# The first layer norm shared between ScalarE and VectorE, the receptance weights split inside the mix, and one block of transposes moved to the head of unit 18

## What is computed

```python
x = L0_attn_x                                   # (1, 2048, 512)
y = _layernorm(x)                               # plain norm
h = _layer_norm(y, ln1_g, ln1_b)                # the norm of the block
hh = _time_shift(h)                             # the token before
r = (h * tm_mr + hh * (1 - tm_mr)) @ Wr.T       # receptance
k = (h * tm_mk + hh * (1 - tm_mk)) @ Wk.T       # key
v = (h * tm_mv + hh * (1 - tm_mv)) @ Wv.T       # value
...
x = y + sigmoid(r) * wkv(k, v) @ Wo.T           # and so on:
                                                # channel mix, then SiLU-gated FFN
```

## Time and profile before

| | us |
|---|---|
| median of three runs | 1042.37 (1040.67 to 1045.35) |
| profiled execution, its own time | 1042.62 |
| its span in the profile | 1040.8 |
| TensorE busy | 1030.8 (99% of the span) |
| VectorE busy | 746.1 (72%) |
| GpSimd busy | 664.5 (64%) |
| ScalarE busy | 538.9 (52%) |

### The profile page before, as it was taken

One profiled execution on the slowest core, in us unless ns is written; L12 is line 12 of the kernel. 1 busy time (PEld: TensorE's weight loads), 2 busy tenths in 40 slices (PEclk: granted clock), 3 DMA queues, 4 the chain that ended last, 5 costly groups with the idle time before them and its releaser, 6 DMA issues.

```text
span 1040.8 us, 13820 instructions
## 1 busy us (share of the span) xinstructions
PE 1030.8 (99%) x4607; PEld 850.6 (82%) x4607; DVE 746.1 (72%) x1240; ACT 538.9 (52%) x902; POOL 664.5 (64%) x541
## 2 busy tenths in 40 slices
PE   8999999999999999999999999999999999999998
PEld 6777888888888888878888888888888888888887
DVE  7899866786576687586568577788689466666655
ACT  7866888857444445355354534333435344444442
POOL 7796673726676875777747565678683456665652
PEclk9999999999999999999999999999999999999999
DMA  9100325367867787989924565964945455445432
GB/s 349 59 21 0 60 66 118 102 204 266 329 219 292 266 277 245 353 310 313 284 99 164 196 227 172 239 236 142 298 164 196 152 169 177 149 153 162 160 103 81
DMA packets 98854, 197.09 MB, mean 189 GB/s; under 512 B 40160, under 2 KB 53344, under 8 KB 93920
## 3 DMA queue, kind: packets, MB, share of 16 engines
q1 hardware_dynamic: 74880, 146.84, 41.3%
q0 software_dynamic: 15168, 48.24, 15.1%
q10 hardware_dynamic: 8736, 1.14, 1.2%
HBM read 117.00 MB, written 74.99 MB: 184 GB/s over the span
## 4 chain that ended last, share of the span: by engine, by line
PE 86%; DVE 5%; POOL 5%; ACT 2%; issue 2%; DMA 0%; SPq 0%; ACTq 0%; DVEq 0%; POOLq 0%
PE bank L941 14%; PE bank L943 14%; PE bank L942 14%; PE bank L930 10%; PE bank L931 10%; PE bank L932 10%; POOL operand L2605 3%; PE bank L1121 2%; PE bank L1122 2%; PE bank L1123 2%; PE bank L1143 2%; PE bank L1141 2%; PE bank L1142 2%; POOL weights L2593 1%; PE bank L1005 1%
## 5 line engine op out<-in xcount | busy, mean ns | idle before, releaser
L941 PE MATMUL bank<-combo,left 128*128 128x512 f32 x672 | 262.2, 390 | 0.4 <-ACT made L1571 0.2
L943 PE MATMUL bank<-combo,left 128*128 128x512 f32 x672 | 261.5, 389 | 0.0
L942 PE MATMUL bank<-combo,left 128*128 128x512 f32 x672 | 261.5, 389 | 0.0
L2640 POOL TENSOR_TENSOR left<-quart,left 128x512 fp32r<-128x512 f32 x96 | 115.9, 1230 | 74.5 <-ACT left L1447 43.4
L941 PEld LDWEIGHTS bank<-combo,left 128*128 128x128 f32 x672 | 126.1, 188 | 28.6 <-ACT bank L1685 0.8
L943 PEld LDWEIGHTS bank<-combo,left 128*128 128x128 f32 x672 | 126.1, 188 | 26.4
L942 PEld LDWEIGHTS bank<-combo,left 128*128 128x128 f32 x672 | 126.1, 188 | 25.9
L2679 POOL TENSOR_TENSOR inner<-made,inner 128x512 fp32r<-128x512 f32 x64 | 86.1, 1368 | 61.6 <-ACT inner L1562 61.5
L2117 DVE TENSOR_TENSOR resid<-bank,resid 128x512 f32<-128x512 f32 x120 | 80.9, 686 | 51.5 <-PE bank L932 50.6
L2605 POOL TENSOR_TENSOR operand<-made,operand 128x512 fp32r<-128x512 f32 x64 | 83.2, 1353 | 34.2 <-ACT operand L1324 34.2
L930 PE MATMUL bank<-right,inner 128*128 128x512 f32 x256 | 99.6, 389 | 0.0
(11 more groups left out here) (232 smaller groups left out, 2364.9 us busy)
## 6 DMA issues: line engine op xcount, KB each, us to landing
kept_left<-left SPq DMA_DIRECT2D x24, 1792.0 KB, 8.6
left<-kept_left POOLq DMA_DIRECT2D x24, 1024.0 KB, 8.1
left<-kept_left POOLq DMA_DIRECT2D x24, 768.0 KB, 4.9
val_w<-kept_w SPq DMA_DIRECT2D x25, 512.0 KB, 5.7
quart<-wide SPq DMA_DIRECT2D x24, 512.0 KB, 3.8
tall_staged<-tall SPq DMA_DIRECT2D x32, 256.0 KB, 4.8
raw<-kept SPq DMA_DIRECT2D x32, 256.0 KB, 8.5
kept_w<-right SPq DMA_DIRECT2D x26, 256.0 KB, 7.1
```

Source lines behind the costliest of these rows:

```text
L941: pe.matmul(acc[:], hi, combo[:, c, k, 0, :], start=fresh and k == 0, stop=False, skip_group_check=True)
L942: pe.matmul(acc[:], hi, combo[:, c, k, 1, :], start=False, stop=False, skip_group_check=True)
L943: mm = pe.matmul(acc[:], lo, combo[:, c, k, 0, :], start=False, stop=k == 1, skip_group_check=True)
L2640: lo = pool.tensor_tensor(left[u % 2][:, 1, a[0]:a[0] + n, :], quart[:, a[0] + 1:a[0] + 1 + n, :], left[u % 2][:, 0, a[0]:a[0] + n, :].bit ...
```

## The change

Seven things are done to the start, and one to units 17 and 18.

1. ScalarE scales tiles 0 and 1 of block 0 (an Identity activation with scale and bias), VectorE only tiles 2 and 3. For the bias VectorE makes `offset1`, one small operation per tile.
2. VectorE's order: the variance of tile 2 comes before the moments of tile 3; the three operations of `shares` for r, k and v stand between the scalings of tile 2 and tile 3.
3. GpSimd waits for other counts of `first_var`, and the first norm's own factor (`first_norm0`) moves behind the four low parts of the r operand.
4. ScalarE makes the high parts of Wr's slices 0 and 1 before the mix and those of slices 2 and 3 inside it (`first_mix`).
5. VectorE makes the low part of Wr's slice 3 behind the four mixes of r, not ahead of them.
6. TensorE's filler transposes go from 19 and 20 to 15 and 18.
7. TensorE waits for tiles 0 and 1 on a semaphore that ScalarE raises.
8. The turning of block 3 moves from the middle of unit 17, ahead of its last product, to the head of unit 18.

```diff
@@ TensorE, first_norm1
-                    pe.wait_ge(z1_ready, s + 1)
+                    if s < 2:
+                        pe.wait_ge(first_z, 1 + s + 1)
+                    else:
+                        pe.wait_ge(z1_ready, 1 if s == 2 else SUBS)
@@ TensorE, unit(u)
                 q = u - GROUP_UNIT
+                if u == KEYS + 2:
+                    turn_value(PAIRS + 1)
                 left_there(0)
...
                 values(5)
-                if u == KEYS + 1:
-                    turn_value(PAIRS + 1)
@@ TensorE
-            keep_running(19)
+            keep_running(15)
             first_norm1()
-            keep_running(20)
+            keep_running(18)
@@ ScalarE
+            def first_norm1():
+                for s in range(2):
+                    act.wait_ge(first_rstd, s + 1)
+                    act.wait_ge(first_var, 3 + 2 * s)
+                    act.activation(resid[:, 0, s, :], resid[:, 0, s, :], ACT.Identity, bias=offset1[:, 0, s:s + 1],
+                                   scale=rstd1[:, 0, 1, s:s + 1]).then_inc(first_z, 1)
+
+            def first_mix():
+
+                rest_of("r", 0, 0)
+                rest_of("r", 0, 1)
+                place_free("r", 0)
+                operand_hi("r", 0, 0)
+                rest_of("r", 0, 2)
+                operand_hi("r", 0, 1)
+                matrix_hi(ITEM_R, range(2, 3))
+                rest_of("r", 0, 3)
+                operand_hi("r", 0, 2)
+                matrix_hi(ITEM_R, range(3, KT))
+                operand_hi("r", 0, 3)
+                matrix_hi(ITEM_K, range(1))
...
-            matrix_hi(ITEM_R)
+            first_norm1()
+            matrix_hi(ITEM_R, range(2))
             act.wait_ge(const_done, 3)
-            mixed("r", 0, behind=1, amid=lambda: matrix_hi(ITEM_K, range(1)))
+            first_mix()
@@ VectorE, first_norm1
                 summed(0)
-                for s in range(1, SUBS):
-                    summed(s)
-                    varied(s - 1)
-                varied(SUBS - 1)
-                for s in range(SUBS):
-                    normed(s)
+                summed(1)
+                varied(0)
+                summed(2)
+                varied(1)
+                offset(0)
+                varied(2)
+                summed(3)
+                offset(1)
+                varied(3)
+                normed(2, 1)
+                shares(slice(0, 3), 0)
+                normed(3, SUBS - 1)
                 dve.tensor_scalar(var_eps[:, 0], stats1[:, 0, :, 1], EPS, None, ALU.add).then_inc(first_var, 1)
-                shares(slice(0, 3), 0)
@@ VectorE
             first_norm1()
-            last_of_r_lo()
             dve.wait_ge(const_done, 7)
             mix("r", 0)
+            last_of_r_lo()
@@ GpSimd
             def first_norm1():
-                for s in range(SUBS):
-                    pool.wait_ge(first_var, s + 1)
+                for s, done in enumerate((1, 2, 4, 6)):
+                    pool.wait_ge(first_var, done)
                     pool.tensor_tensor(rstd1[:, 0, 1, s:s + 1], var_eps[:, 1, s:s + 1], minus_half[:, 1, s:s + 1],
                                        ALU.pow).then_inc(first_rstd, 1)
-                pool.wait_ge(first_var, SUBS + 1)
+
+            def first_norm0():
+                pool.wait_ge(first_var, 7)
                 pool.tensor_tensor(rstd1[:, 0, 0], var_eps[:, 0], minus_half[:, 0], ALU.pow).then_inc(first_rstd, 1)
@@ GpSimd
             matrix_lo(ITEM_R, range(KT - 1))
             operand_lo("r", 0)
+            first_norm0()
             operand_lo("k", 0)
```

12 lines of the change are left out of this document (9 added, 3 removed).

## The result

| | before | changed |
|---|---|---|
| median of 22 runs, us | 1042.73 (1040.67 to 1045.35) | 1045.67 (1043.21 to 1047.47) |
| profiled execution, its own time | 1042.62 | 1044.37 |
| its span | 1040.8 | 1042.6 |

The ratio is 1.0024, with a 95% interval of 1.0018 to 1.0030: the changed kernel is about 2.5 us slower (1.9 to 3.1). The forecast was 1.1 us slower, and no change by the bound of 0.5%. The sign and the bound held; the size is over twice what was forecast. The two medians lie 2.9 us apart, within the interval. The changed median of 1045.67 us is at the very edge of the stated range (1041.1 to 1045.7 us) and outside the likeliest case (1042.6 to 1044.6 us). The upper end of that range had been set for a late clock, which is not what this profile shows, so that the number still fell inside owes something to luck.

What follows compares the result with a forecast made beforehand. GpSimd's k operand, not TensorE's earlier start, was taken to bound the start. +1.3 us past 60 us and -0.2 us in unit 18 gave +1.1 us: 1043.5 us against the runs, range 1041.1 to 1045.7 us.

Steps and rivals of the forecast that it cites:

- the bound of 0.5%: Whole kernel: a measurement tells about 0.5%, 5.2 us, from no change; chance 0.95 of staying within it.
- the likeliest case: Whole kernel: GpSimd's later k operand outweighs unit 18's gain, about 1.1 us slower, 1042.6 to 1044.6 us; chance 0.5.
- a late clock: First transposes: fewer fillers raise TensorE's clock late, 0.8 us longer; 1044.3 to 1046 us, chance 0.15; more, 0.03.
- coming back: After the k operand: closing later GpSimd waits recover a little of the 1.6 us delay, leaving +1.3 us past 60 us.

Runs made afterwards that it cites:

- hi2_early: Changed kernel, but ScalarE makes the high part of Wr's slice 2 before its first high part of the operand: median 1043.92 us, ratio to before 1.0015.
- best3: Changed kernel with Wr's high parts 0 to 2 before the mix, 3 inside, and VectorE's slice 3 low part between second and third mix: 1042.62 us, ratio 0.9999.
- turn_only: Kernel before with only the turning of block 3 moved to unit 18's head: median 1042.39 us, ratio to before 0.9996.
- before_again: Kernel before, unchanged, measured once more for scatter and a second profile: median 1042.52 us, ratio 0.9995.

## What to carry to other kernels

An engine that is on the critical path by its queue pays for every operation put into it and for every wait for a helper, however small; count where its last result lands, not where its first begins. Count the other ways to its inputs too: once GpSimd's queue was free, it stood waiting for VectorE and ScalarE, so the prices of the moves don't add up. Don't credit a delay with coming back unless a wait on the same chain is tied to something that doesn't shift, such as a transfer. And a wait that seems idle may be what keeps two engines from meeting: without it, and with the factor moved, the start was 2.6 us late here (1.84 against 0.75 us where the wait alone differs), where I had expected a gain.

## What the runs showed that I had not expected

- Small VectorE operations beside GpSimd's subtractions: 0.16 us can become 1.25 us, and four scalings of 1.91 us become 3.88 us.
- GpSimd's own small factor takes 1.01 us alone and 1.46 us amid VectorE's subtractions (hi2_early, best3); beside VectorE's mixes, which read a bank, it took 1.02 us (changed).
- One product on VectorE takes 0.68 or 2.10 us in two executions of the same program.
- Tile 3's moments begin between 6.28 and 7.53 us in fourteen executions, and with the old start the share near 58 us moves by as much (turn_only, before_again).
- TensorE's transposes start 0.21 or 0.11 us apart, by when the clock rises; in fourteen executions that was from before the first tile's transposes to about 10.1 us.
